# Two-layer graph attention: blocks of 30 edge tiles with a node range of their own in place of node windows with 36 tile places

## What is computed

```python
# layer 0
score = einsum('ehd,ehd->eh', q[dst], k[src]);  score = clip(score / sqrt(HD), -10, 10)
ex = exp(score - smax[dst]);  alpha = ex / segment_sum(ex, dst)[dst]
y = segment_sum(alpha[:, :, None] * v[src], dst).reshape(n, C) @ Wp.T + bp
x = x + y;  x = x + gelu(layernorm(x) @ W1.T + b1) @ W2.T + b2      # and a residual and layernorm
# layer 1
z = leaky_relu((x @ W_s.T)[src] + (x @ W_t.T)[dst]);  e = z @ W_attn.T
alpha = exp(e - m[src]) / segment_sum(exp(e - m[src]), src)[src]
out = layernorm(x + segment_sum(x[src] * alpha[:, None], dst) @ W_fc.T + b_fc)
```

## Time and profile before

| what | us |
|---|---|
| median of three runs | 4420.28 |
| the profiled execution | 4421.56 |
| its span | 4419.7 |
| PE busy | 2636.1 (60%) |
| DVE busy | 2387.9 (54%) |
| POOL busy | 2389.6 (54%) |
| ACT busy | 1328.2 (30%) |
| granted PE clock, mean | 0.753 of full |
| DMA | 708 MB, 160 GB/s |

### The profile page before, as it was taken

The page is one execution under the profiler, slowest core; times in us unless marked ns, Lnnn a source line. Parts: engine busy times, 40 slices in busy tenths (PEclk is TensorE's granted clock), DMA queues, the critical chain, the costliest instruction groups (busy, mean ns, idle before and its releaser), DMA issues. The chain is left out here.

```text
span 4419.7 us, 59683 instructions
## 1 busy us (share of the span) xinstructions
PE 2636.1 (60%) x12270; PEld 1915.8 (43%) x12271; DVE 2387.9 (54%) x6515; ACT 1328.2 (30%) x3525; POOL 2389.6 (54%) x2340
## 2 busy tenths in 40 slices
PE   5666666666666666884333333333333695777776
PEld 2344444444444445663122222222222594656565
DVE  4555555555555553442444444444445665666665
ACT  0355555554555553331122222222222100111111
POOL 0455555555555552113666666666666474666664
PEclk9788878787887778987666666666666556988988
DMA  3555655555565553114666666666667104655655
GB/s 129 157 172 172 176 169 170 174 170 165 172 172 172 171 171 66 48 48 131 185 191 189 187 191 192 194 194 194 195 194 191 40 0 141 194 191 191 195 190 166
DMA packets 347135, 708.07 MB, mean 160 GB/s; under 512 B 81680, under 2 KB 217797, under 8 KB 347102
## 3 DMA queue, kind: packets, MB, share of 16 engines
q0 software_dynamic: 151200, 472.92, 37.6%
q1 hardware_dynamic: 188840, 223.45, 16.2%
q10 hardware_dynamic: 7062, 11.34, 0.7%
HBM read 625.16 MB, written 82.35 MB: 160 GB/s over the span
## 5 line engine op out<-in xcount | busy, mean ns | idle before, releaser
L747 PE MATMUL ps_px<-sb_parts,sb_bits 128*128 x5400 | 987.0, 345 | 1004.2 <-DVEq L1422 666.9
L619 POOL DMA_INDIRECT sb_ring<-kv_rows,sb_idx x900 | 883.8, 982 | 775.8 <-DVE sb_msg L1291 406.9
L747 PEld LDWEIGHTS ps_px<-sb_parts,sb_bits 128*128 128x128 bf16 x5400 | 635.1, 122 | 1372.1 <-DVEq L1422 613.3
L761 PE MATMUL ps_pa<-sb_msg,sb_onehot 128*128 128x264 f32 x1800 | 642.8, 491 | 391.0 <-DVE sb_msg L1291 345.0
L988 ACT ACTIVATE sb_bits<-sb_bits 128x256 bf16<-128x256 bf16 x900 | 361.2, 409 | 1051.5 <-remote 668.8
L1276 DVE TENSOR_TENSOR sb_prod<-ps_px,sb_ring 128x512 f32<-128x512 f32 x450 | 309.8, 688 | 648.9 <-remote 405.6
L761 PEld LDWEIGHTS ps_pa<-sb_msg,sb_onehot 128*128 128x128 f32 x1800 | 387.8, 239 | 531.8 <-DVE sb_msg L1291 367.4
L619 POOL DMA_INDIRECT sb_ring<-proj_rows,sb_idx x300 | 286.9, 956 | 270.3 <-DMA sb_idx<-in_src 100.9
L619 POOL DMA_INDIRECT sb_w<-narrow_rows,sb_idx x300 | 288.1, 960 | 169.9 <-DVEq L1422 87.6
L1425 DVE SCALAR_TENSOR_TENSOR sb_prod<-sb_msg,sb_attn_hi 128x256 f32<-128x256 f32 x900 | 334.3, 420 | 1.5 <-DVE sb_prod L1425 0.8
L1291 DVE TENSOR_TENSOR sb_msg<-sb_ring,sb_msg 128x512 f32<-128x512 f32 x450 | 308.3, 685 | 0.2 <-issue 0.2
(11 more groups left out here) (220 smaller groups left out, 3760.0 us busy)
## 6 DMA issues: line engine op xcount, KB each, us to landing
sb_bits<-dst_short SPq DMA_DIRECT2D x304, 192.0 KB
x_edges<-sb_ring SPq DMA_DIRECT2D x50, 768.0 KB
sb_slots<-x_edges SPq DMA_DIRECT2D x50, 768.0 KB
x_edges<-sb_slots SPq DMA_DIRECT2D x25, 768.0 KB
sb_w<-x_edges SPq DMA_DIRECT2D x25, 768.0 KB
sb_msg<-lo_rows SPq DMA_DIRECT2D x26, 576.0 KB
sb_ring<-kv_rows,sb_idx POOLq DMA_INDIRECT x900
kv_rows<-sb_slots ACTq DMA_DIRECT2D x25, 256.0 KB, 2.0
```

The costliest lines, as they stand in the source:

```text
L619: pool.indirect_dma_start(out=out[:, i, :], out_offset=None, in_=rows, in_offset=bass.IndirectOffsetOnAxis(ap=idx[:, 2 * p + i:2 * p + i + ...
L747: mm = pe.matmul(px[:, j, 0:width], onehot_t[:, j, :], flat(parts[:, bass.ds(w, 1), a, 0:width]), start=(a == 0), stop=(a == 2))
L761: mm = pe.matmul(pa[:, 0:C + H], onehot[:, j, :], msg[:, j, :], start=False, stop=True, skip_group_check=True)
```

## The change

- A visit has G = 30 tiles (15 pairs) in place of 36. Its nodes are no longer a fixed window: block k has the tiles 30k to 30k + 29, and its 125 nodes start at the smallest destination in it. A test on the chip (`worst`) asks that every block spans at most 125 nodes and that the ranges leave no gap; if so there are BLOCKS = 27 visits, if not, 25 windows of 125 nodes are visited as before, with 30 tiles a visit.
- A node may lie in two blocks. The sums are carried by a one-hot matmul that shifts them to the next block's places (`shift_hot`, `sums_carried`, `agg_carried`); the opening matmul with zeros is gone.
- The ring of gathered k/v rows has 5 pairs in place of 6; DVE's product buffer has 3 places in place of 2. Rows of destinations have 5 buffers in place of 2 and are loaded a visit ahead; those of the second pass, and its indices, before the node stage.
- The bf16 parts of the nodes go to DRAM (`part_rows`, 990 KB for five windows), and each visit loads its 128 nodes (`node_parts`), one visit ahead, into one of two buffers. The projected sums of a visit are stored (`products_out`), and loaded by batches in the node stage (`load_sums`).
- x1 is loaded after the second edge pass. In the final pass its rows come by visit (`features`), and each visit's output is stored by itself (`output_out`).
- Of a visit's 30 tiles, 18 have full rows in the second pass and are streamed in the final one (pairs 0 to 2, 6 to 8, 12 to 14), 12 are gathered.
- Denominators: blocks of DT = 31 tiles, 26 of them; all three products on DVE in one instruction; low one-hot as weights (128 columns), 75 columns streamed; the features are multiplied and stored in five pieces.

The diff, cut:

```diff
-G = 36
-S = 12
+WN = N_NODES // W
+G = 30
+S = 10
...
-VISITS = 578
...
-DT = 26
+DT = 31
...
-        prod = sb("prod", [P, 2, 2 * C])
+        prod = sb("prod", [P, 3, 2 * C])
...
+
+        def streamed(p):
+            return p // RING % 2 == 0
...
-        def streamed(p):
-            return p % SLOTS < RING
+        def chunk(p):
+            return p // (2 * RING)
...
+                def node_parts(node, parity):
+                    sp.dma_start(visit_parts[:, bass.ds(parity, 1), :, 0:width].rearrange("p o a c -> p (o a) c"),
+                                 part_rows[bass.ds(node, P), :, 0:width]).then_inc(node_in[L], 16)
...
+                def products_out(v):
+                    node = visit_value(sp, "node", v)
+                    sp.wait_ge(wp_act, v * 2 + 3)
+                    sp.sem_inc(sp_seen, 1)
+                    sp.wait_ge(y_stored, v * 16 + 1)
+                    sp.sem_inc(sp_seen, 1)
+                    sp.dma_start(y_rows[bass.ds(node, P), :], y_stage).then_inc(y_stored, 16)
...
-                        if h + 2 < HALVES:
-                            rows(tile, h + 2)
-                        else:
-                            rows(after, h + 2 - HALVES)
+                        rows(after, h)
...
+                            fetched(v, range(h // 2 * SLOTS, h // 2 * SLOTS + SLOTS))
                             indices(after, h // 2)
-                for c in range(THIRDS):
-                    sp.wait_ge(idx_in[L][c], total * 16 + 16)
+                        if h == 0:
+                            sp.wait_ge(expd[L], v * PAIRS + RING)
+                            sp.sem_inc(sp_seen, 1)
+                            sp.wait_ge(node_in[L], v * 16 + 16)
+                            sp.sem_inc(sp_seen, 1)
+                            node_parts(node, parity)
+                        if L == 0 and h == 3 and earlier is not None:
+                            products_out(earlier)
...
+            def load_sums(it):
+                sp.dma_start(y_batch, y_rows[bass.ds(it * (NB * P), NB * P), :].rearrange("(w p) c -> p w c", p=P)).then_inc(y_in, 16)
...
+            def store_parts(it):
+                sp.wait_ge(split_v, (W // NB + it) * SPLITS + SPLITS + 1)
+                sp.sem_inc(sp_seen, 1)
+                sp.dma_start(part_rows[bass.ds(it * (NB * P), NB * P), :, :].rearrange("(s p) a c -> p s (a c)", p=P),
+                             parts[:, 0:NB].rearrange("p s a c -> p s (a c)")).then_inc(part_out, 16)
...
-            sp.dma_start(x1, proj_rows[:, CW:ROW].rearrange("(w p) c -> p w c", p=P)).then_inc(x1_back, 16)
-            edge_pass(1)
...
+            sp.sem_inc(sp_seen, 1)
+            sp.dma_start(x1, proj_rows[:, CW:ROW].rearrange("(w p) c -> p w c", p=P)).then_inc(x1_back, 16)
...
             def indices(tile, c):
-                sp.dma_start(idx[:, c * S + R:(c + 1) * S], io["src"][:, bass.ds(tile + c * S + R, R)]).then_inc(idx_in[2][c], 16)
-
-            fetch, value = visit_registers(sp, "sp2")
+                at, n = 2 * GATHERED[c][0], 2 * len(GATHERED[c])
+                sp.dma_start(idx[:, at:at + n], io["src"][:, bass.ds(tile + at, n)]).then_inc(idx_in[2][c], 16)
...
+            def features(v):
+                node = visit_value(sp, "node", v)
+                sp.dma_start(x1_rows, proj_rows[bass.ds(node, P), CW:ROW]).then_inc(x1_row_in, 16)
...
+            def output_out(v):
+                node = visit_value(sp, "node", v)
+                sp.wait_ge(gv, v * GV + GV)
+                sp.sem_inc(sp_seen, 1)
+                sp.wait_ge(out_stored, v * 16 + 1)
+                sp.sem_inc(sp_seen, 1)
+                sp.dma_start(io["out"][bass.ds(node, WN), :], out_stage[0:WN, :]).then_inc(out_stored, 16)
...
-            pool.wait_ge(dsplit, 5)
-            with pool.Fori(0, TD // DT // 2) as it:
-                for b in range(2):
-
-                    pool.wait_ge(dh, it * 2 + b + 1)
-                    t0 = it * (2 * DT) + b * DT
-                    for a in range(2):
-                        pool.tensor_tensor(hi_ex[:, b, a * W:(a + 1) * W], hi_hot[:, b],
-                                           e_parts[:, a, bass.ds(t0, DT)].unsqueeze(1).broadcast_to([P, W, DT]), ALU.mult).then_inc(dx, 1)
-            pool.wait_ge(feat_stored, 16)
+            pool.wait_ge(feat_stored, 16 * NB)
             gathers_x()
...
+            def expand(L, width, parity, v, p):
+
+                if p == 0:
+                    pe.wait_ge(node_in[L], v * 16 + 16)
                 pe.wait_ge(hot_t[L], v * PAIRS + p + 2)
...
-                        mm = pe.matmul(px[:, j, 0:width], onehot_t[:, j, :], flat(parts[:, bass.ds(w, 1), a, 0:width]),
+                        mm = pe.matmul(px[:, j, 0:width], onehot_t[:, j, :], flat(visit_parts[:, bass.ds(parity, 1), a, 0:width]),
...
-            def open_group(width, v):
-
-                pe.wait_ge(opened, v + 1)
-                pe.matmul(pa[:, 0:width], zeros[:, 0:P], zeros[:, P:P + width], start=True, stop=True, skip_group_check=True)
...
-                    mm = pe.matmul(pa[:, 0:C + H], onehot[:, j, :], msg[:, j, :], start=False, stop=True, skip_group_check=True)
+                if p == 0:
+                    pe.wait_ge(opened, v + 1)
+                for i, j in enumerate(flight(p)):
+                    mm = pe.matmul(pa[:, 0:C + H], onehot[:, j, :], msg[:, j, :], start=(p == 0 and i == 0), stop=True, skip_group_check=True)
                 mm.then_inc(summed, 1)
+
+            def sums_carried(v):
+
+                pe.wait_ge(nd, v * ND + NDS["shift"])
+                pe.matmul(pa[:, 0:C + H], shift_hot[:], agg[:], start=False, stop=True, skip_group_check=True)
...
                     if earlier is not None and p == 1:
                         sums_transposed(earlier)
+                        sums_carried(earlier)
...
             pe.wait_ge(ea, 1)
-            pe.matmul(pn[0:3 * W, 0:P], zeros[:, 0:3 * W], zeros[:, P:2 * P], start=True, stop=True, skip_group_check=True)
+            pe.matmul(pn[:, 0:3 * W], zeros[:, 0:P], zeros[:, P:P + 3 * W], start=True, stop=True, skip_group_check=True)
             with pe.Fori(0, TD // DT // 2) as it:
                 for b in range(2):
                     pe.wait_ge(dv, it * 2 + b + 1)
-                    pe.wait_ge(dx, it * 4 + 2 * b + 2)
                     for j in range(DT):
-                        mm = pe.matmul(pn[0:3 * W, 0:P], hi_ex[:, b, :, j], lo_hot[:, b, :, j],
+                        mm = pe.matmul(pn[:, 0:3 * W], lo_hot[:, b, :, j], hi_ex[:, b, :, :, j].rearrange("p a n -> p (a n)"),
                                        start=False, stop=True, skip_group_check=True)
                     mm.then_inc(dpe, 1)
-            pe.wait_ge(fv, FVS["d75"])
-            pe.matmul(pn[:, P:P + W], d75[:], pick[:], start=True, stop=True).then_inc(fpe, 1)
...
+            def agg_carried(v):
+                pe.wait_ge(dgs, v * len(DGS) + DGS["shift"])
+                pe.matmul(pa[:, 0:C], shift_hot[:], agg[:, 0:C], start=False, stop=True, skip_group_check=True)
...
+            def split(rows, width, base, stored):
+
+                dve.wait_ge(part_out, stored * 16 + 1)
+                dve.sem_inc(dve_seen, 1)
...
+                act.dma_start(part_rows[bass.ds(it * (NB * P), NB * P), :, :].rearrange("(s p) a c -> p s (a c)", p=P),
+                              parts[:, 0:NB].rearrange("p s a c -> p s (a c)")).then_inc(part_out, 16)
...
-                dve.scalar_tensor_tensor(out=agg[:], in0=agg[:], scalar=carried[:, bass.ds(v, 1)], in1=pa[:, 0:C + H],
-                                         op0=ALU.mult, op1=ALU.add).then_inc(nd, 1)
+                dve.tensor_copy(agg[:], pa[:, 0:C + H]).then_inc(nd, 1)
...
+                dve.tensor_scalar(shift_hot[:], iota[:], moved[:, bass.ds(v + 1, 1)], None, ALU.is_equal).then_inc(nd, 1)
...
-                    dve.tensor_tensor(hi_ex[:, b, 2 * W:3 * W], hi_hot[:, b],
-                                      e_parts[:, 2, bass.ds(t0, DT)].unsqueeze(1).broadcast_to([P, W, DT]), ALU.mult).then_inc(dv, 1)
+                    dve.tensor_tensor(hi_ex[:, b], hi_hot[:, b].unsqueeze(1).broadcast_to([P, 3, W, DT]),
+                                      e_parts[:, :, bass.ds(t0, DT)].unsqueeze(2).broadcast_to([P, 3, W, DT]), ALU.mult).then_inc(dv, 1)
             dve.wait_ge(dpe, TD // DT + 2)
-            dve.tensor_copy(d75[:], pn[0:3 * W, 0:P]).then_inc(fv, 1)
-            dve.wait_ge(fpe, 1)
-
-            dve.tensor_scalar(denom[:, 0], pn[:, P:P + W], 0.0, None, ALU.is_equal).then_inc(fv, 1)
+            dve.tensor_reduce(dsum[:], pn[:, 0:3 * W].rearrange("p (a w) -> p w a", a=3), AX, ALU.add).then_inc(fv, 1)
+            dve.wait_ge(fv, FVS["dsum"])
...
-            dve.tensor_tensor(feats[:], x1, denom[:, 2].unsqueeze(2).broadcast_to([P, W, C]), ALU.mult).then_inc(fv, 1)
+            for i in range(NB):
+                some = slice(i * W // NB, (i + 1) * W // NB)
```

(19 more changed lines are left out.)

503 lines of the change are left out of this document (305 added, 198 removed).

## The result

The changed kernel takes 4056.27 us (median of four runs, 4047.44 to 4065.03), the kernel before 4420.39: ratio 0.9175, 95% interval 0.9151 to 0.9199. The forecast was 4138, the range 3930 to 4320. The profiled execution spans 4050.9 us, 368.8 less than before; the forecast sum was 281.

A forecast was written before the change was run, and what follows sets the result against it. No engine was full; all three passes were taken to pay per tile place. Terms summing to -281 us took the 4419.7 us span to 4138.7, forecast 4138, with a range of 3930 to 4320 for 8 in 10.

The forecast's parts named there:

- The core: All three passes pay per tile place; places fall from 900 to 810, so 405 pairs for 450.
- First pass, -153 for -85: First edge pass: fewer pairs shorten it by 85 us, the middle taken between two cases, -154 and -8.
- the first one: First edge pass: a pair still costs 3.43 us, 1389 us against 1543, -154 us.
- the other case: First edge pass: bursts shrink with the ring, the pause stays, 3.79 us a pair, 1535 us, -8 us.
- slots bind: Rival, first edge pass: five slots give three pairs per 13.87 us cycle, 4.62 a pair, +329; total 4552 us; chance 0.11.
- Denominators, -78 for -17: Denominators: swapped operands make the matmul cheaper, -25 us (between -6 and -68), and the x1 wait adds 8.
- The wait for x1: Start of the denominators: DVE waits for the x1 load, now issued after the last expansion; +8 us, bounds 0 and +14.
- Second pass, -86 for -100: Second edge pass: fewer pairs at nearly the old cost per pair save 100 us, bounds -140 and 0.
- bytes bind: Rival: bytes set the time, so the second pass gains nothing and the final pass only 20 us; total 4287; chance 0.14.
- Final pass, -45 for -74: Final pass: 27 visits of 24 us, 1.28 times PE's 18.5, save 69 us; storing features in pieces saves 5.
- Setup, node stage, start and tail: Outside the passes: setup +12 us, node stage +5, start of the second pass -12, tail -10.

The follow-up runs named there:

- e10: Changed kernel with a 15-pair first-pass ring, earlier index loads in both edge passes, later x1 wait, earlier first sums load: 3938.35 us, ratio 0.9038 to before.
- e3: Changed kernel with a ring of 3 pairs of gathered rows in the first edge pass in place of 5: 5576.73 us.
- e1: Changed kernel with the denominators' matmul operands turned back (75 columns as weights, 128 streamed), products still on DVE: 4120.14 us, before 4424.7.
- e11: Changed kernel, ring of 5 kept, earlier index loads in the second edge pass, later x1 wait, earlier first sums load: 3323.59 us, ratio 0.9004 to before.
- e6: Changed kernel with the final pass's output stores and x1 row loads on ACT's queue in place of SP's: 3359.47 us, before 3693.24.
- e12: e11 with the final pass's output stores and x1 row loads on ACT's queue: 3328.03 us, ratio 0.9025 to before.
- e5: Changed kernel with two thirds of the next visit's indices loaded earlier in SP's queue in the second edge pass: 3341.84 us, before 3693.24.
- e2: Changed kernel with two of the denominators' three products back on POOL, operands still swapped: 4092.56 us.

## Why the prediction came out

**The core was right.** Time goes with the tile places: 405 pairs for 450, at 3.44 us for 3.43 in the first pass, 3.25 for 3.12 in the second, 1.65 for 1.60 in the final one. The gain was larger than the sum by 88 us: two terms were too small, by 68 (first pass) and 61 (denominators), two too large, by 14 (second pass) and 29 (final pass). That the total lies within 82 us of the forecast is in part luck: the errors offset each other.

**First pass, -153 for -85: a term mis-sized.** Of the two cases I had taken the middle, and the first one (a pair costs what it did) was the truth. The step that failed is the other case: "the burst shrinks with the ring, three pairs per 7.5 + 3.87 us". The burst did shrink: counted over POOL's gathers as above (from 200 us on), before there are 61 bursts of eight and 32 of six, after 37 and 62. But the pause after a burst of six is shorter too. In the trace of before it averages 2.95 us, with 10.48 us for three pairs, 3.49 each; after eight 3.62, 13.78 for four, 3.44. In the changed kernel a pair costs 3.51 and 3.43. I had read one burst and carried its pause over; the bursts of six stood in the trace that I had. The waits in the first pass, beside the earlier trace rows:

```profile
POOL sb_ring L759 <- DVE sb_msg L1458: 377.5, 164, 4.4
...
DVE sb_prod L1443 <- remote: 339.9, 89, 4.9
```

The pairs fell by 10%, POOL's waits by 7%, DVE's by 16%. The rival "slots bind" is out by the cost of a pair itself (3.44 us for its 4.62), and for the ring as a limit by e10 (fifteen slots gain nothing where before takes 4360); e3 agrees (by its loop five slots need 2.4 us a pair). On the faster chips, where a pair costs 2.81, a larger ring does gain: there the slots do bind a little.

**Denominators, -78 for -17: the cost of the matmul.** I bounded it by 182 us (columns add up) and 120 (DVE bounds) and took 25 of the 68 between. The loop went to DVE's bound: from 198.0 us (3471.58 to 3669.60) to 116.6 (3240.76 to 3357.38), 4.5 a block. DVE's 4.6 us a block came out as 0.58 + 2.29 + 1.41 of work. e1 shows that the old operands alone bring PE back to 0.220 us a tile. The 128-column loads take 8.15 / 62 = 0.131 us, the 75-column ones took 0.224: more columns, loaded faster. By the rule on weights of exactly 128 columns in the Trainium skill ("TensorE: Matmul & The Clock Gate", section "Weight-path perf modes — Fast Weight Load (FWL) and DoubleRow"), the trace agrees, and the sum would have been 43 us nearer. I had this in the text and gave it no weight. What the runs don't separate is the faster load from the shorter stream, since they came together. In both forms the mean load is nearly the whole cost of a tile (0.224 of 0.226 us before, 0.131 of 0.136 after), which points to the load. The wait for x1 was 6.70 us for the 8 forecast.

**Second pass, -86 for -100.** By count it would be -140. POOL's waits for indices (139.2 us in 22 pieces; before, 15.3 in 4) took 52 of it, by e10 on another chip of the slower kind. They came with the change's new order in SP's queue, which the sum had left out. The rival "bytes bind" is out: 203 GB/s after, 216 in e10, both above the 191 of before, and 259 on the chip of e11.

**Final pass, -45 for -74.** The visit cost 24.7 us for 24, and there are 27 of them. The fullest engine was forecast rightly: PE has 450 of the 610 us from 3400 to 4010, 18.2 a visit for 18.5. What failed is the factor from it to the visit, carried over as 1.28 from a pass that POOL filled; it came out as 24.7 / 18.2 = 1.36. POOL has 12 gathers, and waits for indices there too:

```profile
POOL sb_w L759 <- DMA sb_idx<-in_src: 111.3, 14, 11.2
```

They stand in SP's queue behind the output of the visit before; I had called that queue "hidden while each has 20 us". Before, POOL waited 0.3 us for indices in this pass. As the same kind of wait cost 52 us in the second pass, it is the likeliest cause here; but e6 and e12 ran where these waits are under 20 us and can't say, so it isn't shown.

**Setup, node stage, start and tail** came each within 3 us of the sum, though with parts that cancel. Between the passes, the first addition came 11 us later and the second pass started 16 us earlier.

## What to carry to other kernels

A pause seen once is not a constant: count how a burst and its pause occur over the whole stage before carrying one to another size. Where two engines and a matmul share a loop, removing one limit may give little, and removing the next all of it; so price the edits together (12 and 33 us alone, 78 both). An experiment that removes a wait says something only where the wait is: e5, e6 and e12 ran on chips that hardly have it. A transfer moved earlier in a queue delays whatever stands behind it: the rows preloaded for the second pass held up the load of the sums by 4 us (1565.92 to 1570.15).

## What the runs showed of the hardware

- The same kernel took 4420, 4425, 4360, 3693 and 3690 us on the occasions of this study. In the changed kernel and its variants the denominators' stretch was 149 us on the slower kind and 153 on the faster where its loop is unchanged (145 on both with the wait for x1 moved), the way from POOL's first addition to the first score of the second pass 333 to 338 us on both, and gathers in a row started every 1.25 us on both. What differs by more than a few microseconds is the edge passes and the final pass: 51.5 for 42.2 us a visit, 9.74 for 7.65 us for three pairs, 24.7 for 18.3 us a visit. On the faster chips DVE's waits of the kind "remote" are gone, and it waits for gathers instead, as here in e11's first pass (beside the rows above):

```profile
DVE sb_prod L1449 <- DMA sb_ring<-kv_rows,sb_idx: 279.8, 214, 3.2
...
POOL sb_ring L765 <- DVE sb_msg L1464: 174.1, 241, 2.1
```

- On the slower kind of chip, while POOL issues gathers one after another, DVE stood up to 18.5 us for a pair whose expansion was done and whose gathers had been issued 22 us before (e10, above). That a signal is held back is inferred; what holds it back, and why not on the others, is open.
- A DVE instruction of 0.58 us takes 1.8 us beside a POOL multiply (e2), as 0.49 became 1.63 in the earlier trace rows.
- In the denominators the granted clock was 0.50 of full, the 1.2 GHz level, before and after, with PE busy over 90% of the time (178.3 of 180 us from 3480 to 3660 before, 107.5 of 115 after).
